# First attention of a four-layer block: where the causal mask is added, and wide score tiles in two pieces

## The chip, the cores and the metric

The kernel is one program on one core of a Trainium2 chip. The metric is the device time of one execution in microseconds. Engines named below: TensorE (PE) does matrix products and transposes, its operands come from SBUF and its results go to PSUM, which has eight banks of 512 float32 columns on each of 128 partitions; VectorE (DVE), ScalarE (ACT) and GpSimd (POOL) work element by element; SyncE (SP) issues the transfers. Each engine works through its own queue in order, and the queues are tied together by semaphores: an instruction waits until a semaphore has reached a number, and increments one when it is done.

## The reference

Four layers are applied to x of shape (2, 1024, 128), each as x + norm(layer(norm(x))), where norm is a layer norm without gain: an attention with rotary positions, a gated feed-forward of ternary weights, a differential attention with 8 heads, and a mixture of 8 experts. Only the first matters here:

```python
Q = jnp.einsum('btd,ed->bte', x, Wq)
K = jnp.einsum('btd,ed->bte', x, Wk)
V = jnp.einsum('btd,ed->bte', x, Wv)
Qr = _rotate(Q, cos, sin)
Kr = _rotate(K, cos, sin)
scores = jnp.einsum('bqd,bkd->bqk', Qr, Kr) / jnp.sqrt(jnp.float32(d))
mask = jnp.tril(jnp.ones((T, T), dtype=bool), k=1)
scores = jnp.where(mask[None, :, :], scores, -jnp.inf)
attn = jax.nn.softmax(scores, axis=-1)
out = jnp.einsum('bqk,bkd->bqd', attn, V)
```

The mask lets a query see all keys up to one beyond its own position (k=1). T is 1024 and d is 128.

## The kernel before

The first attention (stage a) works on 16 query tiles t of 128 rows, eight per batch; i = t mod 8 is the place of a tile in its batch. By the mask, tile i sees 128(i + 1) + 1 keys (at most 1024), so the width of its scores grows from 129 to 1024 columns. The scores of a tile lie in two neighbouring PSUM banks (0 and 1 for even t, 2 and 3 for odd t), so tiles with i of 4 and above reach well into the second bank, and tile i = 3 reaches into it by one column.

For each tile the work goes round four engines:

- TensorE, `a_scores(t)`: the product of rotated queries and keys, one per bank (L558), and over the last 129 columns (128 for i = 7) a product of a bfloat16 identity with the mask (L561), which adds -1e30 to the forbidden keys while the bank's accumulation is open. It waits for the rotation (`ropeq`, `ropek`) and for the exponentials of tile t - 2, which shared the banks.
- VectorE, `a_max(t)`: the row maximum over the whole width (L1322), then its multiple with the negative scale (L1323), the bias of the exponential.
- ScalarE, `a_exp(t)`: one exponential over the whole width with the row sum as a second output (L992).
- TensorE, `a_turn(t)`: i + 1 transposes of 128x128 into banks 4 and 5 (L574); ScalarE, `a_turned(t)`: a copy of them to SBUF (L1002); TensorE, `a_values(t)`: i + 1 products with the values (L587); VectorE, `a_next(t)` (L1334, L1335: the probability of the one key beyond the tile, and the reciprocal of the row sum) and `a_post(t)` (L1343, L1346: adding that key's value, and scaling the row).

The order on each engine is written out by hand. In step t TensorE does the scores of t, the transposes of t - 1 and the value products of t - 2; VectorE does `a_next(t - 2)`, `a_max(t)`, then `a_post(t - 2)`; ScalarE does the copy of t - 1 and the exponential of t. Into this order the remaining projections of the input (TensorE and ScalarE, t = 0 to 4), the rotation (VectorE at t = 0, 1, 4, 5, L1286 to L1307, and GpSimd for the second batch, L1849 and L1857) and the statistics and norms of finished rows (VectorE L1240 and L1243, GpSimd L1828 to L1831, ScalarE L979 after the exponentials of t = 7, 12, 13 and 15) are placed. `me.step` issues a VectorE instruction and waits for its end; `me.mark` issues it only. The helper `mm` is TensorE's matmul.

Of the kernel before, what the change touches and what calls it, by code (L numbers as in the profile page):

```python
# [18 lines left out]
BF16 = mybir.dt.bfloat16  # L19
I32 = mybir.dt.int32  # L20
ALU = mybir.AluOpType
# [3 lines left out]
P = 128  # L25
BATCH, SEQ = 2, 1024
TILES = BATCH * SEQ // P
BT = SEQ // P
# [114 lines left out]
def sandwich(nc, x_in, a_w, rope, b_w12, b_h1, b_h2, b_w3, b_s, b_s3, c_w, c_wo, c_bo, small,  # L143
             d_wg, d_wu, d_wd, d_wr, ident_in, ident_bf_in, mask_in, before_in, out):
    with ExitStack() as ctx:
        def sb(name, shape, dt=F32):
            return ctx.enter_context(nc.sbuf_tensor(name, shape, dt))
# [12 lines left out]
        ident = sb("ident", [P, P])  # L160
        ident_bf = sb("ident_bf", [P, P], BF16)
        mask = sb("mask", [P, P + 1], BF16)
# [42 lines left out]
        tiny = sb("tiny", [P, 64])  # L205
        nlam = sb("nlam", [P, 1])
        cs_tab = sb("cs_tab", [P, 2, CT, HEADS, 2])
        raw = sb("raw", [P, 2, CHUNK])
# [114 lines left out]
        def rotated(b, i):  # L323
# [3 lines left out]
            return 2 * b + (2 if P * (i + 1) < CHUNK else 3)  # L327

        def att_width(i):

            return min(P * (i + 1) + 1, SEQ)
# [28 lines left out]
        def _(sp):  # L360
# [6 lines left out]
            for c in range(2, CHUNKS):  # L367
                sp.dma_start(x[:, chunk(c), :], x_src[:, chunk(c), :]).then_inc(ld[f"x{c}"], 16)
            sp.dma_start(ident_bf[:], ident_bf_in).then_inc(ld["con"], 16)
            sp.dma_start(mask[:], mask_in).then_inc(ld["con"], 16)  # L370
# [117 lines left out]
        def _(pe):  # L488
# [46 lines left out]
            def a_scores(t):  # L535
                b, i = divmod(t, BT)
                base = 2 * (t % 2)
                if t == 0:
                    pe.wait_ge(ld["con"], 32)
                    pe.wait_ge(S["q_made"], 1)  # L540
                if t == 1:
                    pe.wait_ge(S["q_made"], 2)
                if t == 3:
                    pe.wait_ge(S["k_made"], 3)
                if t == 4:
                    pe.wait_ge(S["q_made"], CHUNKS)
                seen = rotated(b, i)
                pe.wait_ge(S["ropeq"], seen)
                pe.wait_ge(S["ropek"], seen)
                if t >= 2:  # L550
                    pe.wait_ge(S["e_a"], t - 1)
                w = att_width(i)
                for n0 in range(0, w, CHUNK):
                    n1 = min(w, n0 + CHUNK)
                    m0, m1 = max(n0, P * i), n1
                    bank = base + n0 // CHUNK
                    masked = m1 > m0
                    last = mm(ps[:, bank, 0:n1 - n0], q_t[:, b, i * P:(i + 1) * P], k_t[:, b, n0:n1],  # L558
                              start=True, stop=not masked)
                    if masked:  # L560
                        last = mm(ps[:, bank, m0 - n0:m1 - n0], ident_bf[:],  # L561
                                  mask[:, m0 - P * i:m1 - P * i], start=False, stop=True)
                last.then_inc(S["s_a"], 1)

            def a_turn(t):
                i = t % BT
                pe.wait_ge(S["e_a"], t + 1)
                if t == 0:
                    pe.wait_ge(S["vout"], 2)
                if t == 4:  # L570
                    pe.wait_ge(S["vout"], CHUNKS)
                pe.wait_ge(S["pe_a"], t)
                for j in range(i + 1):
                    last = nc.tensor.transpose(ps[:, 4 + j // CT, (j % CT) * P:(j % CT + 1) * P],  # L574
                                               probs[:, t % 2, j * P:(j + 1) * P], ident[:])
                last.then_inc(S["pt_a"], 1)
# [362 lines left out]
        def _(act):  # L939
# [46 lines left out]
            def a_exp(t):  # L986
                w = att_width(t % BT)
                act.wait_ge(S["m_a"], t + 1)
                if t >= 2:
                    act.wait_ge(S["pt_a"], t - 1)  # L990
                base = 2 * CHUNK * (t % 2)
                A(probs[:, t % 2, 0:w], banks[:, base:base + w], ACT.Exp, bias=nmx[:, t:t + 1],  # L992
                  scale=ATT_SCALE, accum_out=rsum[:, t:t + 1]).then_inc(S["e_a"], 1)

# [209 lines left out]
        def _(dve):  # L1204
# [113 lines left out]
            def a_max(t):  # L1318
                w = att_width(t % BT)
                dve.wait_ge(S["s_a"], t + 1)  # L1320
                base = 2 * CHUNK * (t % 2)
                me.step(v.tensor_reduce(mx[:, t:t + 1], banks[:, base:base + w], AX.X, ALU.max))  # L1322
                v.tensor_scalar(nmx[:, t:t + 1], mx[:, t:t + 1], -ATT_SCALE, None, ALU.mult).then_inc(S["m_a"], 1)  # L1323

# [4 lines left out]
            def a_next(t):  # L1329

                dve.wait_ge(S["e_a"], t + 1)
                w = P * (t % BT + 1)
                if t % BT < BT - 1:
                    me.mark(v.tensor_copy(p_next[:, t:t + 1], probs[:, t % 2, w:w + 1]))  # L1334
                me.step(v.reciprocal(rinv[:, t:t + 1], rsum[:, t:t + 1]))  # L1335

# [765 lines left out]
```

## Time and profile before

| | us |
|---|---|
| median of 3 runs (703.64 to 704.94) | 703.73 |
| the profiled execution | 704.66 |
| its span | 702.9 |
| TensorE busy | 634.1 |
| VectorE busy | 528.9 |
| ScalarE busy | 489.2 |
| GpSimd busy | 188.3 |

The span runs from the first to the last instruction that the profiler saw; the execution's time has a little around it. A row of a timeline has the start in us from the span's start, the duration in us (from the first start to the last end where several instructions are merged as xN), the engine, the line of the kernel, the operation, output and inputs by name with their shapes, and in brackets the idle time before it and what ended that. Neighbouring instructions on an engine can overlap a little, so that durations do not add up exactly. A row of the grouped view has the group's busy time, the mean duration of one in ns and the idle time before it. Of these, only the stretch up to about 72 us belongs to the first attention.

### The profile page before, as it was taken

What the parts mean: (1) busy time and instruction counts of PE and PEld (TensorE: products, weight loads), DVE (VectorE), ACT (ScalarE), POOL (GpSimd) and SP (SyncE); (2) the same over time, 40 slices, a digit from 0 to 9 for tenths busy, and PEclk for the clock granted to TensorE, in tenths of its full rate; (3) what the DMA queues carried; (4) which work ended last, traced back from release to release, by engine and by line L of the source; (5) the groups of instructions that cost most, each with busy time, mean ns of one, the idle gap of its engine ahead of it and who ended that gap; (6) DMA issues with size and microseconds to landing.
All of it is one profiled execution on the core that took longest, in us unless ns stands there. A gap on an engine that the chain in (4) does not pass through costs nothing.

```text
span 702.9 us, 9405 instructions
## 1 busy us (share of the span) xinstructions
PE 634.1 (90%) x3324; PEld 272.4 (39%) x3324; DVE 528.9 (75%) x993; ACT 489.2 (70%) x503; POOL 188.3 (27%) x250
## 2 busy tenths in 40 slices
PE   7989899999999899889988888898898788899996
PEld 4677345464464423223222112122231111266555
DVE  6876512427155399999899999999999999676775
ACT  4656324225333499999999999999999989444431
POOL 4532240212102041491148101705600006022012
PEclk9999999999999999999999999999999989999999
DMA  5430200002204301234013510111102103300171
GB/s 171 134 137 1 92 1 0 2 0 59 77 1 137 111 11 47 57 105 138 5 57 97 151 56 11 49 57 56 31 27 57 56 3 120 119 1 1 41 232 30
DMA packets 33230, 44.60 MB, mean 63 GB/s; under 512 B 5408, under 2 KB 20000, under 8 KB 32800
## 3 DMA queue, kind: packets, MB, share of 16 engines
q1 hardware_dynamic: 33184, 44.01, 21.1%
q8 instruction: 26, 0.43, 0.3%
q14 instruction: 20, 0.16, 0.1%
HBM read 31.60 MB, written 10.55 MB: 60 GB/s over the span
## 4 chain that ended last, share of the span: by engine, by line
PE 43%; ACT 23%; DVE 21%; issue 11%; POOL 1%; DVEq 0%; ACTq 0%
ACT w_hh L1138 19%; PE ps L778 8%; PE ps L788 8%; DVE hid L1482 5%; DVE hid L1477 5%; PE ps L813 5%; PE ps L760 4%; PE ps L690 3%; PE ps L671 3%; PE ps L744 2%; PE ps L822 2%; ACT probs L1109 2%; DVE st L1240 2%; PE ps L587 1%; PE ps L493 1%
## 5 line engine op out<-in xcount | busy, mean ns | idle before, releaser
L1138 ACT ACTIVATE w_hh<-hid 128x2048 f32<-128x2048 f32 x128 | 249.9, 1952 | 8.3 <-DVE hid L1482 7.8
L690 PE MATMUL ps<-w_hh,v_h 128*32 128x512 f32 x1024 | 137.8, 610 | 33.4 <-ACT w_hh L1138 32.3
L1477 DVE TENSOR_TENSOR hid<-ps,probs 128x1024 f32<-128x1024 f32 x86 | 104.5, 1215 | 19.4 <-ACT probs L1109 16.1
L671 PE MATMUL ps<-q_s,k_s 64*128 64x512 bf16 x256 | 99.3, 389 | 14.7 <-DVE hid L1477 14.1
L1482 DVE SCALAR_TENSOR_TENSOR hid<-ps,probs 128x1024 f32<-128x1024 f32 x86 | 104.7, 1217 | 4.6 <-PE ps L671 3.3
L671 PE MATMUL ps<-q_w,k_w 64*128 64x512 bf16 x256 | 99.4, 389 | 0.0
L1109 ACT ACTIVATE probs<-ps 128x1024 f32<-128x1024 f32 x86 | 91.3, 1062 | 2.2 <-PE ps L671 2.2
L671 PE MATMUL ps<-q_g,k_s 128*128 128x512 bf16 x256 | 78.3, 388 | 1.1 <-ACT qkv_a L1109 1.1
L671 PEld LDWEIGHTS ps<-q_w,k_w 64*128 64x128 bf16 x256 | 23.7, 92 | 107.2 <-issue 55.3
L788 PE MATMUL ps<-hid,w_hh 128*128 128x512 f32 x128 | 56.3, 592 | 0.0
L778 PE MATMUL ps<-hid,w_hh 128*128 128x512 f32 x128 | 55.8, 594 | 0.0
L1477 DVE TENSOR_TENSOR hid<-ps,qkv_a 128x1024 f32<-128x1024 f32 x42 | 51.0, 1215 | 2.7 <-ACT w_hh L1138 1.8
L1482 DVE SCALAR_TENSOR_TENSOR hid<-ps,qkv_a 128x1024 f32<-128x1024 f32 x42 | 51.2, 1218 | 2.0 <-PE ps L671 1.7
L1173 ACT ACTIVATE q_g<-ps 128x512 f32<-128x512 f32 x32 | 19.1, 598 | 45.5 <-PE ps L813 45.4
L671 PEld LDWEIGHTS ps<-q_s,k_s 64*128 64x128 bf16 x256 | 23.7, 92 | 63.2 <-DVE hid L1477 35.1
L1822 POOL TENSOR_SCALAR rs<-mv 128x4 f32<-128x4 f32 x18 | 5.2, 289 | 160.1 <-DVE mv L1243 160.0
L690 PEld LDWEIGHTS ps<-w_hh,v_h 128*32 128x32 f32 x1024 | 20.7, 108 | 69.1 <-ACT w_hh L1138 50.4
L1109 ACT ACTIVATE qkv_a<-ps 128x1024 f32<-128x1024 f32 x42 | 44.6, 1063 | 2.6 <-PE ps L671 2.6
L1379 DVE SCALAR_TENSOR_TENSOR hid<-ps,s_b,rot 128x512 f32<-128x512 f32 x16 | 11.9, 750 | 42.8 <-ACT rot L1075 42.8
L1093 ACT ACTIVATE hid<-ps,s_b 128x512 f32<-128x512 f32 x16 | 11.0, 687 | 43.9 <-PE ps L788 43.9
L1891 POOL TENSOR_SCALAR v_h<-v_c 128x128 f32<-128x128 f32 x16 | 8.5, 535 | 113.5 <-PE ps L690 113.4
L778 PEld LDWEIGHTS ps<-hid,w_hh 128*128 128x128 f32 x128 | 24.0, 190 | 30.2 <-issue 29.4
(314 smaller groups left out, 1001.2 us busy)
## 6 DMA issues: line engine op xcount, KB each, us to landing
qk_rows<-part SPq DMA_DIRECT2D x48, 128.0 KB, 2.4
w_hh<-w_rows SPq DMA_DIRECT2D x4, 1024.0 KB, 8.8
qk_rows<-part_g SPq DMA_DIRECT2D x24, 128.0 KB, 2.4
q_g<-qk_rows SPq DMA_DIRECT2D x32, 96.0 KB, 2.2
k_s<-qk_rows SPq DMA_DIRECT2D x32, 96.0 KB, 2.3
q_s<-qk_rows SPq DMA_DIRECT2D x32, 96.0 KB, 2.4
k_w<-qk_rows SPq DMA_DIRECT2D x32, 96.0 KB, 2.5
q_w<-qk_rows SPq DMA_DIRECT2D x32, 96.0 KB, 2.4
```

What stands on the lines that cost most here:

```text
L671: last = mm(ps[:, base + half, :], k_op[rows, u, keys], q_op[rows, u, half * CHUNK:(half + 1) * CHUNK], start=True, stop=True)
L690: last = mm(ps[VW * g4:VW * g4 + VW, 6, :], v_h[:, u, mt, :], ee[:, mt % 2, g4 * CHUNK:(g4 + 1) * CHUNK], start=(mt == 0), stop=(mt == BT ...
L744: last = mm(bank[:, k4 * P:(k4 + 1) * P], hid[:, 2, k, k4 * P:(k4 + 1) * P], w_3[:, k, :], start=(k == 0), stop=(k == KT_ - 1))
L760: last = mm(ps[:, 2 * (m % 2) + w, :], w_12[:, w, m * P:(m + 1) * P], xt[:], start=True, stop=True)
L778: last = mm(ps[:, o, :], w_h1[:, k, o * P:(o + 1) * P], hid[:, 0, k, :], start=(k == 0), stop=(k == KT_ - 1))
L788: last = mm(ps[:, o, :], w_h2[:, k, o * P:(o + 1) * P], hid[:, 1, k, :], start=(k == 0), stop=(k == KT_ - 1))
L813: last = mm(ps[:, 2 * (n % 2) + w, :], wt[:, e, :], xt_d[c], start=True, stop=True)
L1109: A(gg[s % 3], banks[:, 0:2 * CHUNK], ACT.Tanh).then_inc(S["g"], 1)
L1138: A(ee[:, mt % 2, :], zz[:, mt % 2, :], ACT.Exp).then_inc(S["e"], 1)
L1173: A(sg_d[:, n % 2, :], ps[:, 2 * (n % 2), :], ACT.Silu).then_inc(S["sg_d"], 1)
L1477: v.tensor_tensor(zz[:, mt % 2, 0:SEQ], banks[:, 2 * CHUNK:4 * CHUNK], gg[s % 3], ALU.add).then_inc(S["z1"], 1)
L1482: v.scalar_tensor_tensor(zz[:, mt % 2, SEQ:2 * SEQ], banks[:, 4 * CHUNK:6 * CHUNK], -1.0, gg[s % 3], ALU.mult, ALU.subtract).then_inc(S["z ...
```

## The change

The mask is no longer added by TensorE. VectorE adds it to the scores in PSUM, in place, over the last 128 or 129 columns, and then takes the maximum. The bfloat16 identity and its load go. Tiles with i of 4 and above are treated as two pieces, bank one and the rest: TensorE signals the first bank's product apart from the second's; VectorE takes one maximum of each piece and joins them in the operation that scales; ScalarE does two exponentials with a row sum each; TensorE's first four transposes wait for the first exponential only; VectorE adds the two row sums in `a_next`. The semaphores `s_a` and `e_a` now count pieces. The norms of this stage are on ScalarE in both versions.

```diff
+        mx_1, rsum_1 = tiny[:, 0:TILES], tiny[:, TILES:2 * TILES]
...
+        def pieces(t):
+
+            return 2 if t % BT >= CT else 1
+
+        def pieces_to(t):
+            return sum(pieces(u) for u in range(t + 1))
...
-            sp.dma_start(ident_bf[:], ident_bf_in).then_inc(ld["con"], 16)
...
-                    pe.wait_ge(ld["con"], 32)
...
-                    pe.wait_ge(S["e_a"], t - 1)
+                    pe.wait_ge(S["e_a"], pieces_to(t - 2))
                 w = att_width(i)
                 for n0 in range(0, w, CHUNK):
                     n1 = min(w, n0 + CHUNK)
-                    m0, m1 = max(n0, P * i), n1
-                    bank = base + n0 // CHUNK
-                    masked = m1 > m0
-                    last = mm(ps[:, bank, 0:n1 - n0], q_t[:, b, i * P:(i + 1) * P], k_t[:, b, n0:n1],
-                              start=True, stop=not masked)
-                    if masked:
-                        last = mm(ps[:, bank, m0 - n0:m1 - n0], ident_bf[:],
-                                  mask[:, m0 - P * i:m1 - P * i], start=False, stop=True)
+                    last = mm(ps[:, base + n0 // CHUNK, 0:n1 - n0], q_t[:, b, i * P:(i + 1) * P], k_t[:, b, n0:n1],
+                              start=True, stop=True)
+                    if n0 == 0 and pieces(t) == 2:
+                        last.then_inc(S["s_a"], 1)
                 last.then_inc(S["s_a"], 1)
...
-                pe.wait_ge(S["e_a"], t + 1)
+                pe.wait_ge(S["e_a"], pieces_to(t) - pieces(t) + 1)
...
                 for j in range(i + 1):
+                    if j == CT:
+                        pe.wait_ge(S["e_a"], pieces_to(t))
...
-                A(probs[:, t % 2, 0:w], banks[:, base:base + w], ACT.Exp, bias=nmx[:, t:t + 1],
-                  scale=ATT_SCALE, accum_out=rsum[:, t:t + 1]).then_inc(S["e_a"], 1)
+                for i, total in enumerate((rsum, rsum_1)[0:pieces(t)]):
+                    n0, n1 = i * CHUNK, w if i == pieces(t) - 1 else CHUNK
+                    A(probs[:, t % 2, n0:n1], banks[:, base + n0:base + n1], ACT.Exp, bias=nmx[:, t:t + 1],
+                      scale=ATT_SCALE, accum_out=total[:, t:t + 1]).then_inc(S["e_a"], 1)
...
             def a_max(t):
                 w = att_width(t % BT)
-                dve.wait_ge(S["s_a"], t + 1)
                 base = 2 * CHUNK * (t % 2)
-                me.step(v.tensor_reduce(mx[:, t:t + 1], banks[:, base:base + w], AX.X, ALU.max))
-                v.tensor_scalar(nmx[:, t:t + 1], mx[:, t:t + 1], -ATT_SCALE, None, ALU.mult).then_inc(S["m_a"], 1)
+                if pieces(t) == 2:
+                    dve.wait_ge(S["s_a"], pieces_to(t) - 1)
+                    me.mark(v.tensor_reduce(mx_1[:, t:t + 1], banks[:, base:base + CHUNK], AX.X, ALU.max))
+                n0 = CHUNK * (pieces(t) - 1)
+                dve.wait_ge(S["s_a"], pieces_to(t))
+                if t == 0:
+                    dve.wait_ge(ld["con"], 16)
+                seen = banks[:, base + P * (t % BT):base + w]
+                me.step(v.tensor_tensor(seen, seen, mask[:, 0:w - P * (t % BT)], ALU.add))
+                me.step(v.tensor_reduce(mx[:, t:t + 1], banks[:, base + n0:base + w], AX.X, ALU.max))
+                if pieces(t) == 2:
+                    v.tensor_scalar(nmx[:, t:t + 1], mx[:, t:t + 1], mx_1[:, t:t + 1], -ATT_SCALE,
+                                    ALU.max, ALU.mult).then_inc(S["m_a"], 1)
+                else:
+                    v.tensor_scalar(nmx[:, t:t + 1], mx[:, t:t + 1], -ATT_SCALE, None, ALU.mult).then_inc(S["m_a"], 1)
...
-                dve.wait_ge(S["e_a"], t + 1)
+                dve.wait_ge(S["e_a"], pieces_to(t))
                 w = P * (t % BT + 1)
                 if t % BT < BT - 1:
                     me.mark(v.tensor_copy(p_next[:, t:t + 1], probs[:, t % 2, w:w + 1]))
+                if pieces(t) == 2:
+                    me.step(v.tensor_tensor(rsum[:, t:t + 1], rsum[:, t:t + 1], rsum_1[:, t:t + 1], ALU.add))
                 me.step(v.reciprocal(rinv[:, t:t + 1], rsum[:, t:t + 1]))
```

What stands on VectorE in the step t = 7, before: `a_next(5)`, `a_max(7)`, `a_post(5)` (mx is the maximum, nmx its scaled negative, rsum the row sum, rinv its reciprocal).

```order
L1334 COPY p_next<-probs 128x1 [waits e_e_a]
L1335 RECIPROCAL rinv<-rsum 128x1
L1322 TENSOR_REDUCE mx<-ps 128x1 [waits e_s_a,self_dve]
L1323 TENSOR_SCALAR nmx<-mx 128x1 [waits self_dve]
L1343 SCALAR_TENSOR_TENSOR y_a<-hid,p_next,ps 128x128 [waits e_v_next0,e_o_a]
L1346 TENSOR_SCALAR y_a<-y_a,rinv 128x128 [waits self_dve]
```

And in the changed kernel, where tiny holds the first piece's maximum and the second piece's row sum:

```order
L1351 COPY p_next<-probs 128x1 [waits e_e_a]
L1353 TENSOR_TENSOR rsum<-rsum,tiny 128x1
L1354 RECIPROCAL rinv<-rsum 128x1 [waits self_dve]
L1328 TENSOR_REDUCE tiny<-ps 128x1 [waits e_s_a,self_dve]
L1334 TENSOR_TENSOR ps<-ps,mask 128x128 [waits e_s_a]
L1335 TENSOR_REDUCE mx<-ps 128x1 [waits self_dve]
L1337 TENSOR_SCALAR nmx<-mx,tiny 128x1 [waits self_dve]
L1362 SCALAR_TENSOR_TENSOR y_a<-hid,p_next,ps 128x128 [waits e_v_next0,e_o_a]
L1365 TENSOR_SCALAR y_a<-y_a,rinv 128x128 [waits self_dve]
```

Three instructions are new: the addition of row sums, the second maximum and the mask's addition. Tiles with i below 4 get the mask's addition only.

On TensorE, the rows around the transposes of t = 7, before: the scores of t = 8, the transposes, the value products of t = 6.

```order
L558 MATMUL ps<-qkv_a 128x129 [waits e_e_a,e_ropek,e_ropeq]
L561 MATMUL ps<-mask,ident_bf 128x129
L574 MATMUL ps<-ident,probs 128x128 [waits e_pe_a,e_e_a]
L574 MATMUL ps<-ident,probs 128x128 x7
L587 MATMUL ps<-qkv_a,probs_t 128x128 [waits e_y_a,e_pe_a]
```

And in the changed kernel:

```order
L560 MATMUL ps<-qkv_a 128x129 [waits e_e_a,e_ropek,e_ropeq]
L577 MATMUL ps<-ident,probs 128x128 [waits e_pe_a,e_e_a]
L577 MATMUL ps<-ident,probs 128x128 x3
L577 MATMUL ps<-ident,probs 128x128 [waits e_e_a]
L577 MATMUL ps<-ident,probs 128x128 x3
L590 MATMUL ps<-qkv_a,probs_t 128x128 [waits e_y_a,e_pe_a]
```

The mask product is gone, and the eight transposes have two waits for ScalarE instead of one.

## Rows read from the trace of the kernel before

**Rows 1.** Windows: us, busy us of each engine (instructions), granted PE clock, DMA.

```profile
14.00:28.00 14.00, 12.55 (x65) 7.93 (x64) 11.91 (x39) 11.48 (x29) 7.18 (x10) 1.00 0.33 82
28.00:42.00 14.00, 13.16 (x88) 9.97 (x86) 13.34 (x39) 7.48 (x14) 8.25 (x9) 1.00 0.82 275
52.00:62.00 10.00, 9.39 (x56) 6.76 (x57) 8.13 (x36) 8.26 (x19) 2.39 (x6) 1.00 0.00 1
```

**Rows 2.** Timeline of VectorE, 14 to 45 us.

```profile
21.74 1.29 DVE L1301 TENSOR_TENSOR qkv_a<-qkv_a,sq 128x512 f32<-128x512 f32 x2
...
27.28 0.35 DVE L1343 SCALAR_TENSOR_TENSOR y_a<-hid,p_next,ps 128x128 f32<-128x128 f32 x1 [1.65 <-PE ps L587]
...
28.83 0.14 DVE L1334 COPY p_next<-probs 128x1 f32<-128x1 f32 x1
...
40.87 0.15 DVE L1323 TENSOR_SCALAR nmx<-mx 128x1 f32<-128x1 f32 x1
```

**Rows 3.** Grouped view by shape, VectorE: xcount | busy us, mean ns | idle.

```profile
L1335 DVE RECIPROCAL rinv<-rsum 128x1 f32<-128x1 f32 x16 | 2.4, 152 | 0.0
L1322 DVE TENSOR_REDUCE mx<-ps 128x1 f32<-128x1024 f32 x2 | 2.4, 1224 | 0.1
L1322 DVE TENSOR_REDUCE mx<-ps 128x1 f32<-128x129 f32 x2 | 0.6, 292 | 0.0
L1561 DVE TENSOR_TENSOR probs_t<-qkv_a,r_o 128x128 f32<-128x128 f32 x2 | 0.5, 283 | 0.0
L1298 DVE TENSOR_TENSOR raw<-ps,tab 128x258 f32<-128x258 f32 x2 | 0.8, 416 | 0.0
```

**Rows 4.** Timeline of TensorE, 14 to 25 us.

```profile
15.87 0.22 PE L561 MATMUL ps<-mask,ident_bf 128*128 128x129 bf16 x1
...
22.78 0.39 PE L587 MATMUL ps<-qkv_a,probs_t 128*128 128x128 f32 x2
23.29 1.10 PE L558 MATMUL ps<-qkv_a 128*128 128x512 f32 x2
24.22 0.22 PE L561 MATMUL ps<-mask,ident_bf 128*128 128x128 bf16 x1
24.28 0.33 PE L558 MATMUL ps<-qkv_a 128*128 128x1 f32 x2
```

**Rows 5.** Timelines of GpSimd and VectorE where one holds up the other.

```profile
34.50 2.88 POOL L1857 TENSOR_TENSOR qkv_a<-qkv_a,part 128x512 f32<-128x512 f32 x2 [0.85 <-DVE part L1307]
...
35.31 0.93 DVE L1346 TENSOR_SCALAR y_a<-y_a,rinv 128x128 f32<-128x128 f32 x1
...
37.99 0.29 DVE L1346 TENSOR_SCALAR y_a<-y_a,rinv 128x128 f32<-128x128 f32 x1
...
55.93 0.24 POOL L1828 TENSOR_SCALAR nb<-mv 128x4 f32<-128x4 f32 x1 [3.17 <-DVE mv L1243]
...
62.01 0.66 DVE L1327 TENSOR_TENSOR x_res<-x_res,y_a 128x512 f32<-128x512 f32 x1
...
62.19 0.58 POOL L1828 TENSOR_SCALAR nb<-mv 128x4 f32<-128x4 f32 x1 [4.31 <-DVE mv L1243]
```

**Rows 6.** Timeline of ScalarE, 27 to 68 us.

```profile
27.36 0.69 ACT L992 ACTIVATE probs<-ps,nmx 128x513 f32<-128x513 f32 x1
27.94 0.21 ACT L992 ACTIVATION_READ_ACCUMULATOR probs<-ps,nmx 128x1 f32 x1
...
41.06 1.11 ACT L992 ACTIVATE probs<-ps,nmx 128x1024 f32<-128x1024 f32 x1 [0.25 <-DVE nmx L1323]
...
42.16 1.64 ACT L979 ACTIVATE y_a<-y_a,nb,rs 128x128 f32<-128x128 f32 x4
...
67.06 1.00 ACT L1002 ACTIVATE probs_t<-ps 128x1024 f32<-128x1024 f32 x1
```

**Rows 7.** Timeline of TensorE, 42 to 70 us.

```profile
42.32 1.09 PE L574 MATMUL ps<-ident,probs 128*128 128x128 f32 x8 [0.84 <-ACT probs L992]
...
58.20 0.87 PE L574 MATMUL ps<-ident,probs 128*128 128x128 f32 x6
...
66.60 3.56 PE L587 MATMUL ps<-qkv_a,probs_t 128*128 128x128 f32 x30
```

**Rows 8.** Timeline of VectorE near 64 us; waits up to 160 us (total, times, longest).

```profile
64.22 0.15 DVE L1323 TENSOR_SCALAR nmx<-mx 128x1 f32<-128x1 f32 x1
...
PEld ps L574 <- ACT probs L992: 6.1, 8, 1.8
...
DVE mx L1322 <- PE ps L561: 0.5, 2, 0.3
```

More of the change, by code:

```diff
@@ L143, in sandwich @@
 def sandwich(nc, x_in, a_w, rope, b_w12, b_h1, b_h2, b_w3, b_s, b_s3, c_w, c_wo, c_bo, small,
-             d_wg, d_wu, d_wd, d_wr, ident_in, ident_bf_in, mask_in, before_in, out):
+             d_wg, d_wu, d_wd, d_wr, ident_in, mask_in, before_in, out):
     with ExitStack() as ctx:
@@ L160, in sandwich @@
         ident = sb("ident", [P, P])
-        ident_bf = sb("ident_bf", [P, P], BF16)
         mask = sb("mask", [P, P + 1], BF16)
@@ L2089 @@
         "d_wd": f["L1_ffn_Wd"].transpose(1, 0, 2), "d_wr": f["L1_ffn_Wr"], "ident": eye,
-        "ident_bf": eye.astype(ml_dtypes.bfloat16), "mask": mask, "before": before,
+        "mask": mask, "before": before,
     }
```

## The prediction

> **What bounds the kernel now.** The change touches the first attention alone, so I asked first where that stage lies and which engine it waits for. It runs over 16 query tiles (t = 0 to 15, eight per batch) from about 16 us to 70 us of the span. The windows view is the first to read: between 28 and 42 us VectorE is busy for 13.34 of 14.00 us, while in 52 to 62 us it is TensorE with 9.39 of 10.00 and VectorE has 8.13 [rows 1]. The timeline of VectorE is the second: from 28.83 us on (the small operations ahead of the maximum of t = 4) up to the end of the scaled maximum of t = 7 at 41.02 us not one row has an idle time behind it [rows 2]. So tiles 4 to 7 run at VectorE's pace, tiles 8 to 15 at that of a ring (scores on TensorE, maximum on VectorE, exponentials on ScalarE, transposes on TensorE) with TensorE nearly full. Behind the stage the order of all engines is unchanged and the next stage starts from the last products, so what the stage loses or gains reaches the end one to one. The granted TensorE clock is 1.00 in every window of the stage [rows 1], so the clock enters neither side.
>
> **The start, t = 0 to 3: +0.4 us.** Each tile gets one VectorE addition of 128x129 in PSUM. No row of before has that form. From below: the slope between the maxima of 129 and 1024 columns is (1224 - 292) / 895 = 1.04 ns a column, and 129 columns at that rate alone are 0.13 us; with the 0.03 us that VectorE takes from one finished operation to a dependent next one, 0.165. From above: an addition of 258 columns out of PSUM, 0.416 us, with the same 0.03, 0.45. I take the nearest in size, an SBUF product of 128x128 at 283 ns, with 0.03: **0.31 us** [rows 3]. (The Trainium skill, Vector Engine (DVE) Microarchitecture Reference, 5.2 Measured stream behaviour on trn2, gives about 75 ns of fixed cost per instruction after overlap, an estimate of 0.21 us here; by it the sum below would be about 1.0 us smaller. The rows speak for more: the 292 ns of the 129-column maximum leave 158 beside its columns, and each addition here is waited for.) The additions of t = 0 and 1 stand ahead of the rotation of rows 512 to 1023, which ends at 23.03 us, and the scores of t = 3 start at 23.29 us on it [rows 2, 4]. That is +0.62, less 0.12 of slack (TensorE's product before ends at 23.17 us), so 0.5; the two mask products of t = 3 go, 0.08 us of TensorE. The value products of t = 1 then end 0.4 later, and VectorE, idle 1.65 us for them [rows 2], absorbs the additions of t = 2 and 3 (0.62).
>
> **Tiles 4 to 7, VectorE's own pace: +2.0 us.** Per tile: the mask addition, 0.31; a second maximum over the same columns in all, which costs its fixed part of 292 - 129 x 1.04 = 158 ns less the 0.07 to 0.08 by which undependent operations overlap, 0.08. Four tiles: 4 x 0.39 = 1.6. In the steps of t = 6 and 7 the sums of the exponentials of t = 4 and 5 are in two parts, and their addition lies between a copy and the reciprocal: an operation of one column, 152 ns as the reciprocal, and 0.03 [rows 3], 0.18 each, 0.36 for two. Nothing covers these, since VectorE has no idle there. That the first maximum may start while TensorE writes the second bank brings nothing here: VectorE comes late to both.
>
> **A port that is held, t = 6: +1.1 us.** At 34.50 us GpSimd starts two additions of 128x512 that end at 37.38 us. VectorE's 128x128 scaling at 35.31 us takes 0.93 us instead of 0.29 and ends when the first of the two has ended; and VectorE's two-input addition at 62.01 us stretches a GpSimd operation from 0.24 to 0.58 us [rows 5]. So operations with two SBUF inputs are among those that exclude GpSimd's. The new addition of t = 4's two sums has two SBUF inputs and comes at 36.30 us in before's time, when GpSimd's second has just begun: it waits until 37.38, 1.1 us, in a stretch without slack. (The Trainium skill, GPSIMD Engine Reference, 1. Specifications, says the same of "two SBUF inputs"; the trace shows it with VectorE as the holder, not yet with one column.) Rows cannot tell whether one column suffices: zero is the other end.
>
> **The handover to the second batch, t = 8 to 11: +0.6 us.** An exponential of 513 columns takes 0.69 us and its sum is out 0.79 us after the start [rows 6]; so with a piece of 512 the transposes of t = 7 can start 0.84 us after 41.06 instead of 1.26 (42.32 [rows 7]). Four of them fill 0.44 us, but the second piece ends at 0.70 + 0.79 = 1.49, so all eight are done at 1.98 instead of 2.19: 0.2 us won. ScalarE pays for it, 1.49 instead of 1.22 us, 0.27, then it does the norm of 1.64 us that stands at 42.16 us [rows 6], and only then the copy of t = 7's transposes and the exponential of t = 8, for which the transposes of t = 8 wait. That returns the 0.2 and 0.1 more. The masks of t = 8 to 10 leave TensorE (0.06 each); the VectorE additions of t = 10 and 11 (0.62), with other VectorE work in between and no idle, stand ahead of the exponential of t = 11. Sum: 0.1 - 0.1 + 0.6.
>
> **The second half, t = 12 to 15: +0.9 us.** TensorE sets the pace, and VectorE's additions of 0.39 first use its idle. At t = 13 the scaled maximum comes 0.40 later, the first piece of the exponential is ready 0.84 us on, and the transposes at 58.20 us [rows 7] end 0.24 later than now. At t = 15 the scaled maximum, now at its end at 64.37 us [rows 8], is late by 0.24 + 0.18 + 0.40 = 0.82. Then ScalarE: two pieces (+0.27), the norm, and the copy of the last transposes from 67.06 us [rows 6] is late by 1.09, so it ends at 69.15. The products on t = 14 (14 of the 30 from 66.60 us [rows 7]) end at about 68.2 now and 68.8 then, so the last 16 wait for that copy: they start at 69.2 instead of 68.25, +0.9.
>
> The dropped load of an identity (32 KB) and its place in the DMA queue are worth nothing: the first mask product runs at 15.87 us [rows 4], behind other work; the mask is in by then.
>
> **The sum.** 0.4 + 2.0 + 1.1 + 0.6 + 0.9 = 5.0 us. The profiled execution took 704.66 us, so it would take 709.7; the median of the runs is 703.73, 0.93 lower, so I predict **708.7 us**.
>
> **Rivals.**
> - *No port wait.* One column does not need GpSimd's port: the sum is 3.9, the time 707.6. For it: rows with one column on VectorE are short everywhere. Against it: the rule is in the kind of operation, not its length.
> - *The addition is dear.* If an operation that reads and writes PSUM costs the upper end (0.45), ten such additions on the path (t = 0, 1, 4 to 7, 10, 11, 13, 15) add 10 x 0.14: 710.1.
> - *The addition is cheap* (0.165): 10 x 0.145 less, 707.2, or 706.1 with no port wait.
> - *Faster: TensorE and the handovers set everything.* The 18 mask products leave TensorE (0.06 us each, as between the starts at 24.22 and 24.28 us, 1.0 in all [rows 4]), the wait of the maxima for them goes (0.5 us [rows 8]), and the handovers of t = 7 and 15 shorten by 0.2 each: 1.9 less, 701.8. For it: TensorE is at 9.39 of 10.00 us in the second half [rows 1], and it waits 6.1 us in all for exponentials [rows 8]. It decides only if VectorE had over 2 us to spare between 28.83 and 41.02 us, and there it has none.
>
> **How the numbers follow.** The forecast has 0.40, no port wait 0.24, dear 0.11, cheap 0.12, faster or level 0.13. A change within 0.2% (1.4 us) can't be told from none. Slower holds all cases but the last: 0.87. The last is split, since VectorE's cost may use up most of that gain: faster 0.08, same 0.05. The range reaches from the cheap case with some of the handover won, 705.3, to just above the dear one, 710.4. Leaving out 701.8 costs 0.13.
>
> **What would show each step.** In the profile after: mask additions of 0.28 to 0.32 us, sixteen; the scores of t = 3 at about 23.8 us; the scaled maximum of t = 7 ending near 44.5 (41.02 + 3.5); one one-column addition of about 1.2 us against seven of 0.15; the last copy out of the transposes ending near 73.3; the stage's last product near 75 instead of 70.2. I am wrong if VectorE shows idle times over 0.2 us in tiles 4 to 7, if the addition is under 0.2 us, or if the following stage starts no later than now.

## The result and the profile after

| | before | after |
|---|---|---|
| median of 4 runs each, us | 704.34 (703.64 to 704.98) | 710.61 (709.40 to 711.76) |
| the profiled execution, us | 704.66 | 711.76 |
| its span, us | 702.9 | 709.9 |

The changed kernel is slower: the ratio is 1.0093, with an interval of [1.0078, 1.0107]. The forecast was 708.7 us with a range up to 710.4. The direction and the places were right; the time is 1.9 us above the forecast and 0.2 us outside the range. Three single executions in the runs below took 891, 1217 and 3400 us; they are left out of every median, and the one of them that was profiled (in r_after) gives no rows.

The page of the kernel after, its first two lines (span; busy time of each engine, share, instructions):

```profile
span 709.9 us, 9416 instructions
...
PE 636.7 (90%) x3306; PEld 273.5 (39%) x3306; DVE 537.2 (76%) x1025; ACT 491.2 (69%) x519; POOL 187.9 (26%) x250
```

VectorE has 8.3 us more than before (537.2 against 528.9). Windows of the kernel after (columns as in [rows 1]): the stretch of tiles 4 to 7, then the end of the stage.

```profile
28.00:45.00 17.00, 13.82 (x85) 9.90 (x84) 16.24 (x47) 8.21 (x20) 9.07 (x10) 1.00 0.67 227
...
72.00:73.00 1.00, 1.00 (x9) 1.00 (x8) 0.00 (x0) 1.00 (x4) 0.00 (x0) 0.67 0.05 16
73.00:74.00 1.00, 1.00 (x7) 1.00 (x7) 0.00 (x0) 0.97 (x2) 0.00 (x0) 0.50 0.00 0
74.00:75.00 1.00, 1.00 (x6) 1.00 (x6) 0.00 (x0) 0.00 (x0) 0.00 (x0) 0.50 0.00 0
75.00:76.00 1.00, 1.00 (x8) 1.00 (x7) 0.80 (x4) 0.00 (x0) 0.00 (x0) 0.62 0.00 0
```

The stretch that took 14 us now takes 17, and VectorE is busy for 16.24 of them: it is still the engine that sets the pace there. New is the last column but two of the lower rows: the granted TensorE clock, 1.00 in the same stage of the kernel before, is 0.50 (1.2 instead of 2.4 GHz) from 73 to 75 us.

VectorE of the kernel after, grouped by shape (as [rows 3]):

```profile
L1334 DVE TENSOR_TENSOR ps<-ps,mask 128x129 f32<-128x129 f32 x14 | 4.1, 295 | 0.5 <-PE ps L560 0.2
...
L1353 DVE TENSOR_TENSOR rsum<-rsum,tiny 128x1 f32<-128x1 f32 x8 | 2.2, 279 | 0.0
...
L1337 DVE TENSOR_SCALAR nmx<-mx,tiny 128x1 f32<-128x1 f32 x8 | 1.7, 214 | 0.3
...
L1340 DVE TENSOR_SCALAR nmx<-mx 128x1 f32<-128x1 f32 x8 | 1.2, 154 | 0.3
```

The mask's addition takes 0.295 us. The scaling that also joins the two maxima takes 0.214 us where the plain one takes 0.154. The addition of two row sums has a mean of 0.279 us, which hides one long one. Timeline of VectorE and GpSimd, 36 to 45 us, where one holds up the other (against [rows 2, 5]):

```profile
36.24 2.88 POOL L1876 TENSOR_TENSOR qkv_a<-qkv_a,part 128x512 f32<-128x512 f32 x2 [1.30 <-DVE part L1312]
...
37.97 1.17 DVE L1353 TENSOR_TENSOR rsum<-rsum,tiny 128x1 f32<-128x1 f32 x1
...
42.83 0.15 DVE L1353 TENSOR_TENSOR rsum<-rsum,tiny 128x1 f32<-128x1 f32 x1
...
44.87 0.21 DVE L1337 TENSOR_SCALAR nmx<-mx,tiny 128x1 f32<-128x1 f32 x1
```

At t = 6 the one-column addition takes 1.17 us and ends at 39.14 us, 0.02 us behind the second of GpSimd's two operations (36.24 + 2.88 = 39.12). The next one, with GpSimd idle, takes 0.15.

TensorE of the kernel after at the scores of t = 3, the transposes of t = 7 and the end of the stage (against [rows 4, 7]), then ScalarE at the exponentials of t = 7 and the last copy (against [rows 6]):

```profile
24.27 1.21 PE L560 MATMUL ps<-qkv_a 128*128 128x512 f32 x4 [0.86 <-DVE qkv_a L1306]
...
45.95 1.32 PE L577 MATMUL ps<-ident,probs 128*128 128x128 f32 x8 [1.31 <-ACT probs L997]
...
70.92 1.32 PE L577 MATMUL ps<-ident,probs 128*128 128x128 f32 x8 [1.88 <-ACT probs L997]
72.08 5.14 PE L590 MATMUL ps<-qkv_a,probs_t 128*128 128x128 f32 x30
77.74 0.66 PE L499 MATMUL ps<-ident,xn 128*128 128x128 f32 x4 [0.52 <-DVE y_a L1365]
```

```profile
45.12 0.69 ACT L997 ACTIVATE probs<-ps,nmx 128x512 f32<-128x512 f32 x1 [1.08 <-DVE nmx L1337]
...
45.80 0.68 ACT L997 ACTIVATE probs<-ps,nmx 128x512 f32<-128x512 f32 x1
...
46.46 1.64 ACT L982 ACTIVATE y_a<-y_a,nb,rs 128x128 f32<-128x128 f32 x4
...
72.97 1.01 ACT L1007 ACTIVATE probs_t<-ps 128x1024 f32<-128x1024 f32 x1
```

In the kernel before, TensorE's transposes of t = 15 and those that start the next stage (L493 there) are:

```profile
65.67 1.09 PE L574 MATMUL ps<-ident,probs 128*128 128x128 f32 x8 [1.59 <-ACT probs L992]
...
70.68 0.66 PE L493 MATMUL ps<-ident,xn 128*128 128x128 f32 x4 [0.52 <-DVE y_a L1346]
```

The last 30 value products take 5.14 us instead of 3.56, in just the stretch with the low clock. The next stage starts with its transposes (L499) at 77.74 us; before, they start at 70.68. Behind that nothing changes: TensorE is busy for 78.64 of 80 us from 73 to 153 us before and from 80 to 160 us after, and the spans differ by 7.0 us, as the starts of the stage behind do by 7.06.

**How the kernels below are compared.** Three points of the timeline cut the stage: the scores of t = 3 (23.29 us before [rows 4]), the scaled maximum of t = 7 (40.87 [rows 2]) and the next stage's transposes (70.68). The first moves by some tenths from execution to execution with the input's transfer: VectorE's statistics of x, which wait for it, start anywhere from 11.35 to 12.30 us in the profiles of this study. The two stretches behind it repeat to 0.02 us where nothing in them is changed (20.60 to 20.62 and 31.74 in the rows below that alter neither), so each can be read apart. The columns of times are in us.

| kernel | scores t = 3 | from there to the scaled maximum of t = 7 | from there to the next stage | low clock at the end |
|---|---|---|---|---|
| before | 23.29 | 17.58 | 29.81 | no |
| after | 24.27 | 20.60 | 32.87 | yes |
| after, second profile (r_after2) | 24.07 | 20.61 | 31.74 | no |
| e_ident | 23.96 | 20.61 | 31.74 | no |
| e_mask | 24.45 | 18.76 | 32.60 | yes |
| e_pieces | 23.38 | 19.41 | 30.46 | no |
| e_port | 23.81 | 19.69 | 32.94 | yes |
| e_twice | 24.60 | 21.93 | 33.31 | no |
| e_warm | 24.30 | 20.61 | 32.35 | no |
| e_warm2 | 24.33 | 20.62 | 31.74 | no |
| e_psum | 23.94 | 16.65 | 30.03 | no |
| e_late | 23.64 | 17.57 | 28.94 | no |
| e_best | 23.20 | 16.65 | 29.09 | no |

### The profile page after: what moved, and what is told of

It is laid out like the page before. It is cut to its first block, busy times and chain, and to the rows that moved or that the text cites. A ratio compares the mean times of both kernels' runs of the same rounds, so it can differ in the third digit from the quotient of the medians.

```text
span 709.9 us, 9416 instructions
## 1 busy us (share of the span) xinstructions
PE 636.7 (90%) x3306; PEld 273.5 (39%) x3306; DVE 537.2 (76%) x1025; ACT 491.2 (69%) x519; POOL 187.9 (26%) x250
## 4 chain that ended last, share of the span: by engine, by line
PE 41%; DVE 25%; ACT 22%; issue 11%; POOL 1%; DVEq 0%; ACTq 0%
ACT w_hh L1143 17%; PE ps L781 8%; PE ps L791 8%; DVE hid L1496 6%; DVE hid L1501 6%; PE ps L816 5%; PE ps L763 4%; PE ps L693 3%; PE ps L674 2%; PE ps L747 2%; PE ps L825 2%; DVE st L1245 2%; ACT probs L1114 1%; PE ps L590 1%; PE ps L499 1%
## 5 line engine op out<-in xcount | busy, mean ns | idle before, releaser
L1501 DVE SCALAR_TENSOR_TENSOR hid<-ps,probs 128x1024 f32<-128x1024 f32 x86 | 104.6, 1217 | 3.9 <-PE ps L674 2.7
```

Source lines behind the costliest of these rows:

```text
L1501: v.scalar_tensor_tensor(zz[:, mt % 2, SEQ:2 * SEQ], banks[:, 4 * CHUNK:6 * CHUNK], -1.0, gg[s % 3], ALU.mult, ALU.subtract).then_inc(S["z ...
```

## The experiments

Twelve runs, in three groups, two of them of the changed kernel itself. The kernel before was run beside each group, with medians of 704.44 (r_after to e_port), 704.35 (e_warm, e_twice, e_psum, e_ident) and 703.74 us (the other four).

**r_after: the changed kernel once more**, as the neighbour of the next three.

> The changed kernel once more, unaltered. Two theories on the 1.3 us by which it was slower than the sum of 5.0. Clock: TensorE's granted clock falls to 0.50 behind the idle time ahead of the transposes of t = 15 and makes the last products of the stage 1.6 us longer (5.14 instead of 3.56 us); where the fall is missing, the execution is 1.6 us shorter. Work: VectorE's and ScalarE's additions cost more than the terms; then the time is the same with or without the fall. Both: ratio to before 1.008 to 1.010. The start of the scores of t = 0, 0.35 us later in the first profile (16.00 against 15.65), is back within 0.1 of before if it was chance in the input's transfer.

Measured: 711.63 us (three executions, 710.66 to 711.88), ratio 1.0093 [1.0077, 1.011]. It has no rows.

**e_mask: the mask on VectorE, no pieces.**

```diff
 def pieces(t):
-    return 2 if t % BT >= CT else 1
+    return 1
```

> The mask addition on VectorE alone: every tile one piece, as before. By my terms: start +0.4, tiles 4 to 7 4 x 0.31 = +1.25, no port wait, t = 8 to 11 +0.6 (no second piece on ScalarE, but VectorE's additions at t = 10 and 11), t = 12 to 15 +0.5: together +2.7 us, ratio 1.004, the scaled maximum of t = 7 ending 1.7 later than before. Rival (the pieces are what costs): +1 us or less.

Measured: 707.84 us, ratio 1.004 [1.0028, 1.0053]: 3.4 us by the medians, 2.8 by the ratio. By the table the stretch up to the scaled maximum of t = 7 is 1.18 longer, a little under four additions with their gaps (4 x 0.325 = 1.30). The end of the stage, TensorE's timeline:

```profile
69.22 1.09 PE L577 MATMUL ps<-ident,probs 128*128 128x128 f32 x8 [1.99 <-ACT probs L997]
70.15 5.14 PE L590 MATMUL ps<-qkv_a,probs_t 128*128 128x128 f32 x30
```

So the low clock does not need the pieces. Its 30 products took the 5.14 us of the kernel after, 1.58 more than before's 3.56. Without that the last stretch would be 31.02, 1.21 longer than before, since the copy that the last 16 read ends 1.46 us after the first product starts (71.61 and 70.15), as it does in the kernel before (68.06 and 66.60), where nothing waits for it.

**e_pieces: the pieces, with the mask still on TensorE.**

```diff
+                    if masked:
+                        last = mm(ps[:, bank, m0 - n0:m1 - n0], ident_bf[:],
+                                  mask[:, m0 - P * i:m1 - P * i], start=False, stop=True)
...
-                me.step(v.tensor_tensor(seen, seen, mask[:, 0:w - P * (t % BT)], ALU.add))
```

> The two pieces alone, the mask on TensorE as before. By my terms: start 0, tiles 4 to 7 4 x 0.08 + 2 x 0.18 + 4 x 0.06 for the scaling with two pointers = +0.9, port wait +1.1, handover -0.2 to +0.3, end +0.4: +2.2 to +2.7 us, ratio 1.0035. Rival (the pieces pay by the shorter handovers, the mask is what costs): 0 or faster. The rest that the two parts alone leave of the whole 6.3 would be what comes of both together, the clock first of all.

Measured: 706.54 us, ratio 1.0029 [1.002, 1.0038]. The middle stretch is 1.83 longer, the last 0.65. VectorE, then TensorE at the end:

```profile
36.55 1.17 DVE L1358 TENSOR_TENSOR rsum<-rsum,tiny 128x1 f32<-128x1 f32 x1
```

```profile
67.57 1.32 PE L586 MATMUL ps<-ident,probs 128*128 128x128 f32 x8 [1.49 <-ACT probs L1006]
68.74 1.73 PE L599 MATMUL ps<-qkv_a,probs_t 128*128 128x128 f32 x14
70.68 2.05 PE L599 MATMUL ps<-qkv_a,probs_t 128*128 128x128 f32 x16 [0.22 <-ACT probs_t L1016]
```

The hold of 1.17 us belongs to the pieces, and so does a wait that before has not: the last 16 products start 0.22 us late, on ScalarE's copy (L1016). The two halves of the change add up: in the middle stretch 1.18 + 1.83 = 3.01 against 3.03 for both, in the last 1.21 + 0.65 = 1.86 against 1.93.

**e_port: the row sums added by an instruction with one stream**, the second sum being its scalar pointer.

```diff
-me.step(v.tensor_tensor(rsum[:, t:t + 1], rsum[:, t:t + 1], rsum_1[:, t:t + 1], ALU.add))
+me.step(v.tensor_scalar(rsum[:, t:t + 1], rsum[:, t:t + 1], rsum_1[:, t:t + 1], None, ALU.add))
```

> The changed kernel with the two row sums added by an operation that takes the second as a per-partition scalar, so that it has one tensor input in SBUF. Port theory: the addition of t = 4's sums takes 0.15 instead of 1.17 us beside GpSimd's second addition, the scaled maximum of t = 7 ends 1.0 us earlier, the time falls by 1.0 us. Rival (the 1.17 us is a wait for something else, or the time is given back at the copy of the transposes): same as the changed kernel within 0.3.

Measured: 709.43 us, ratio 1.0068 [1.0053, 1.0083]; 1.2 us under the changed kernel's 710.61 and 2.2 under the runs beside it. The table says it better: the middle stretch is 0.91 shorter than in the kernel after, and the last is equal to it (32.94 and 32.87, both with the low clock). VectorE:

```profile
37.51 0.20 DVE L1353 TENSOR_SCALAR rsum<-rsum,tiny 128x1 f32<-128x1 f32 x1
```

Same place (GpSimd's two operations run from 35.78 to 38.66 us here), same data, and 0.20 us instead of 1.17 (the rest of its eight pay 0.05 more each). The hold of this operation comes from the second SBUF stream, not from where the instruction stands. The Trainium skill (GPSIMD Engine Reference, 1. Specifications) names "two SBUF inputs" as one of the two cases of contention; the trace agrees, and adds that one column is enough and that the pointer scalar of this operation doesn't count as the second input. A single SBUF tensor is no safe form in general: the 128x128 scaling just ahead (L1365, one tensor and a pointer) takes 0.92 us at 36.60 us in this kernel too, against 0.29 with GpSimd idle.

**e_ident: the dropped load of the identity kept.**

```diff
+            sp.dma_start(ident_bf[:], ident_bf_in).then_inc(ld["con"], 16)
...
-                    dve.wait_ge(ld["con"], 16)
+                    dve.wait_ge(ld["con"], 32)
```

> The changed kernel with the load of the bfloat16 identity kept (nobody reads it). I put the dropped load at nothing: the same time as the changed kernel within 0.5 us. Rival (its place in the queue moved the input's third transfer, which the profile after shows 0.2 us later): 0.3 us faster.

Measured: 709.92 us, ratio 1.0083 [1.0068, 1.0098]; both stretches equal to the second profile of the changed kernel, and the scores of t = 3 at 23.96 us, among those of the kernels with one mask addition and without the load (23.81 to 24.45). The load is worth nothing that shows.

**e_twice: the mask's addition done twice.** A forbidden score gets -2e30 instead of -1e30, and its exponential is zero either way.

```diff
-                me.step(v.tensor_tensor(seen, seen, mask[:, 0:w - P * (t % BT)], ALU.add))
+                for _ in range(2):
+                    me.step(v.tensor_tensor(seen, seen, mask[:, 0:w - P * (t % BT)], ALU.add))
```

> The changed kernel with each mask addition made twice, one behind the other (the forbidden scores get -2e30 instead of -1e30, which changes no output). It prices one addition where it stands. By my terms the second costs what the first did: 0.32 each at t = 0 and 1, 4 to 7, 10 and 11, 13 and 15, ten places, +3.2 us; the scaled maximum of t = 7 ends 1.9 later. Rival (most of the additions lie in VectorE's idle times and the cost of the change is the waits and the clock): +1 us or less.

Measured: 713.29 us, ratio 1.013 [1.0116, 1.0143]: 3.4 us over e_ident of the same group, 2.7 over 710.61. The middle stretch grows by 1.32, four times 0.33; the last by 1.57, between four and five times 0.33 for the eight additions in it. So an addition costs its duration and a gap of 0.03 in full where VectorE sets the pace (t = 4 to 7), and for a little over half of the additions behind that. TensorE waited longest of all here, and the clock stayed high:

```profile
74.17 1.32 PE L577 MATMUL ps<-ident,probs 128*128 128x128 f32 x8 [2.21 <-ACT probs L997]
75.33 1.73 PE L590 MATMUL ps<-qkv_a,probs_t 128*128 128x128 f32 x14
```

**e_warm: four products in TensorE's idle time before the transposes of t = 15**, to keep the clock up.

```diff
+                if t == TILES:
+                    pe.wait_ge(S["e_a"], pieces_to(TILES - 2))
+                    for _ in range(4):
+                        mm(ps[:, 0, :], k_t[:, 1, 0:P], k_t[:, 1, 0:CHUNK], start=True, stop=True)
```

> The changed kernel with four matmuls of 512 columns, whose result nobody reads, on TensorE between the value products of t = 13 and the wait for the first exponential of t = 15, where it stood idle 1.88 us. Clock theory: TensorE's granted clock stays 1.00 there, the 30 last value products take 3.6 instead of 5.14 us, the time falls by 1.4 to 1.6 us (the four take 1.72 us, within the idle time). Rival (the chip lowers the clock at this point for what ran before, or the last products are slow for another reason): the same time, 5 us for the products.

Measured: 710.66 us, ratio 1.0093 [1.0079, 1.0106]. TensorE:

```profile
68.92 3.60 PE L614 MATMUL ps<-qkv_a 128*128 128x512 f32 x8
...
73.23 3.51 PE L590 MATMUL ps<-qkv_a,probs_t 128*128 128x128 f32 x30
```

The experiment was badly sized: a float32 product of 512 columns is two instructions of 0.45 us, so the four filled 3.60 us instead of half of that, and the transposes came 1.4 us late. The clock stayed at 1.00, but that proves little.

**e_warm2: the same with two products**, which fit: 1.88 us, then the transposes 0.17 us behind them.

> As the run with four matmuls on TensorE ahead of the transposes of t = 15, with two. Each had turned out as two instructions of 0.45 us, so that the four took 3.60 us instead of the 1.72 that I had allowed for and made these transposes 1.4 us late; two take 1.8 us, inside the 1.88 of idle time. The granted clock stayed 1.00 and the 30 products took 3.51 us there. Clock theory: the clock stays 1.00, the transposes are not late, and the time is 1.0 to 1.6 us below the changed kernel run beside it (1.6 where each of its executions has the fall, less where some have not). Rival: no difference, the fall being a matter of chance that hits both.

Measured: 710.17 us, ratio 1.0087 [1.0073, 1.01]. The clock was high, and the last stretch is 31.74, to the hundredth that of the changed kernel without the fall; its time is 0.3 us above that one's (r_after2, below), inside the noise. Filling the idle costs nothing in the stage. Whether it keeps a fall away is not shown, since the profile beside it had none.

**r_after2: the changed kernel, in the same group.**

> The changed kernel again, beside the one above. One profile of it had the fall of the clock (0.50 from 72.4 to 75.6 us), another, with one unused load more, had none and a stage 5.6 us longer than before's instead of 6.7. Clock theory: ratio to before 1.008 to 1.010, and, if the profile shows no fall, the first product of the next stage 5.6 us after before's (76.3), if it does, 7.1 (77.8).

Measured: 709.86 us (709.22 to 711.45), ratio 1.0084 [1.007, 1.0098]. TensorE, and a window:

```profile
70.75 1.32 PE L577 MATMUL ps<-ident,probs 128*128 128x128 f32 x8 [1.88 <-ACT probs L997]
71.91 1.73 PE L590 MATMUL ps<-qkv_a,probs_t 128*128 128x128 f32 x14
73.86 2.05 PE L590 MATMUL ps<-qkv_a,probs_t 128*128 128x128 f32 x16 [0.22 <-ACT probs_t L1007]
76.42 0.66 PE L499 MATMUL ps<-ident,xn 128*128 128x128 f32 x4 [0.52 <-DVE y_a L1365]
```

```profile
72.00:74.00 2.00, 1.78 (x16) 1.59 (x15) 0.27 (x1) 1.80 (x4) 0.00 (x0) 1.00 0.03 8
```

The same program, the same idle of 1.88 us, and no fall. The wait of the last 16 products for the copy is here as forecast. So the fall is a matter of the execution. In the changed kernel it costs 32.87 - 31.74 = 1.13 us, less than the 1.6 of the products, since without it these would wait for the copy.

**e_psum: the kernel before, with its rows kept in PSUM between `a_post`'s two instructions.** The scaling then reads PSUM and not SBUF.

```diff
-                    me.step(v.scalar_tensor_tensor(y_a[:, t, :], v_next[:, b, i, :], p_next[:, t:t + 1], o,
+                    me.step(v.scalar_tensor_tensor(o, v_next[:, b, i, :], p_next[:, t:t + 1], o,
...
-                    o = y_a[:, t, :]
```

> The kernel before with one thing changed: the row before scaling (values plus the one key beyond) goes back to PSUM instead of SBUF, so that the scaling reads PSUM. Port theory: the scaling then does not wait for GpSimd's additions: 0.35 instead of 1.25, 0.93 and 0.93 us at t = 3 to 5, and 0.06 dearer in the eleven other tiles. VectorE sets the pace there, so the scaled maximum of t = 7 ends 1.2 to 2.0 us earlier, and the kernel is faster than before by 0.8 to 1.5 us (TensorE has under 1 us to spare there). Rival (TensorE or ScalarE takes over at once, or the PSUM operation waits too): no change within 0.3.

Measured: 703.41 us against 704.35, ratio 0.999 [0.9981, 0.9999]. VectorE:

```profile
31.65 0.35 DVE L1345 TENSOR_SCALAR y_a<-ps,rinv 128x128 f32<-128x128 f32 x1
...
32.53 0.96 DVE L1322 TENSOR_REDUCE mx<-ps 128x1 f32<-128x769 f32 x1 [0.41 <-PE ps L561]
```

The scaling takes 0.35 us at t = 3 to 5, where it takes 0.9 to 1.25 in the kernel before (0.93 in [rows 5]). The middle stretch is 0.93 shorter, though some 2 us of VectorE were freed: the rest became waits for TensorE, the 0.41 above among them. 0.22 of it is given back in the last stretch, so the stage gains 0.7 us, a little under the 0.8 to 1.5 that had been expected.

**e_late: the kernel before, with the statistics and the addition of finished rows moved from VectorE's step 14 to 15, and the last norm on ScalarE behind the last copy.**

```diff
-                if t == 15:
+                if t == TILES:
...
-                if t in (6, 12, 14):
+                if t in (6, 12, 15):
...
-                if t in (8, 14, 17):
+                if t in (8, 15, 17):
```

> The kernel before with the statistics of the rows of t = 8 to 11 and the addition of those of t = 4 to 7 moved on VectorE behind the maximum of t = 15 (from t = 14 to 15), and their norm on ScalarE behind the copy of the last transposes. Ring theory: the scaled maximum of t = 15 then ends about 1.9 us earlier (1.2 of statistics, 0.7 of addition), the exponential of t = 15 is held by the copy of t = 14's transposes instead (63.7), 0.7 us earlier than now, and the kernel is 0.6 to 0.8 us faster. Rival (the stage's last products are held by what moved behind): same within 0.3.

Measured: 703.68 us against 703.74, ratio 0.9992 [0.9983, 1.0001]. In the table the last stretch is 0.87 shorter; the timing, with its interval from -1.2 to +0.1 us, doesn't settle it, and the 0.6 to 0.8 us expected of it stay open.

**e_best: both edits on the kernel before.**

> The same, and the rows before scaling kept in PSUM as in the run that was 0.1% faster: the two gains lie in different halves of the stage and add up: 1.2 to 1.6 us below before, ratio 0.998. Rival: the one takes the other's slack, and the ratio is that of the better alone.

Measured: 702.72 us (701.86 to 703.52, ten runs) against 703.74, ratio 0.9978 [0.9969, 0.9988]. TensorE:

```profile
63.98 1.09 PE L574 MATMUL ps<-ident,probs 128*128 128x128 f32 x8 [0.76 <-ACT probs L992]
...
68.94 0.65 PE L493 MATMUL ps<-ident,xn 128*128 128x128 f32 x4 [0.52 <-DVE y_a L1345]
```

The wait of the last transposes falls from 1.59 to 0.76 us, and the next stage starts 1.74 us earlier than in the kernel before: 0.93 in the middle stretch, 0.72 in the last, 0.09 by the start. It is faster than the kernel before by 0.1 to 0.3%, and so than both kernels.

## Why the prediction was right in its mechanism and wrong in its size

**What bounds the kernel.** Right: tiles 4 to 7 run at VectorE's pace (16.24 of 17.00 us), and what was added to VectorE there is paid nearly in full (1.18 of 1.30 us in e_mask, 1.32 of 1.32 in e_twice). Behind the stage all was shifted one to one.

**The steps that failed** are two: a term put at nothing, and a sum that was too small. The first is the last sentence of the prediction's part on what bounds the kernel: "The granted TensorE clock is 1.00 in every window of the stage [rows 1], so the clock enters neither side." The rows were those of the kernel before, and the conclusion was drawn for both. The mechanism forecast for the end of the stage has TensorE idle ahead of the transposes of t = 15 for longer than the 1.59 us of before; it stood idle for 1.88, and in the profiled execution the clock went to 0.50 between 1 and 2 us after work had begun again. A cost above zero belonged in the range there. In this execution it was 1.13 us. The fall of this one execution is not the whole miss: less 1.13 us it would take 710.63, and the median of the four would be 710.45, still just outside the range. The second step is the sum of the terms, +5.0 us, where the rows without a fall show +5.64; the table below has it by terms. The Trainium skill (TensorE: Matmul & The Clock Gate, Part 1) says that the phase at which the chip looks at activity is not tied to the program and varies from run to run; that fits one program with and without the fall, though no run here shows the cause.

How much of the median it makes is only suggested. Of twelve executions of the changed kernel, three have a mean clock of 0.991 and times of 711.63 to 711.88 us; nine have 0.996 or 0.997 and a median of 710.16. No execution of the kernel before, of 50, is below 0.993. But the mean clock is a weak mark: e_port's profiled execution has the fall at a mean of 0.996, and e_warm's has none at 0.993.

**The terms.** The rows without the fall (31.74) against the forecast:

| term | forecast | measured |
|---|---|---|
| start, up to the scores of t = 3 | +0.4 (scores +0.5) | +0.68 |
| tiles 4 to 7, with the port | +2.0 + 1.1 = 3.1 | +3.03 |
| handover, t = 8 to 11 | +0.6 | +0.76 |
| t = 12 to 15 | +0.9 | +1.17 |
| sum | +5.0 | +5.64 |

- *The price of the mask's addition*: taken 0.31 with its gap, measured 0.295 + 0.03. Right, and both rivals on it (0.45 and 0.165) are out; that the time of the dear one, 710.1, lies nearest the result is chance. The Trainium skill's fixed cost of about 75 ns (Vector Engine (DVE) Microarchitecture Reference, 5.2) gave 0.21; the measurement decides against it for an instruction that is waited for: e_twice shows 0.33 for each further one.
- *The port*: right in place and size (1.17 us for an operation of 0.15, a hold of 1.02 where 1.1 was forecast); e_port takes it away and wins 0.91. The rival without it is out.
- *The start*: measured as the mean of the scores of t = 3 in the seven profiles with one mask addition on VectorE (24.17) less that in the five without (23.49). Counted from the start of VectorE's statistics of x, which takes the input's transfer out, it is 0.69 (12.31 to 12.51 us against 11.63 to 11.93). Two additions with their gaps are 0.65. The forecast took off 0.12 of slack, which the profile of before has and those with a later input don't, and 0.08 for mask products, which lie behind this point.
- *The slack at t = 3*: VectorE's idle of 1.65 us [rows 2] was filled by more than the two additions. The scaling of t = 1 now takes 1.09 us (at 25.55 us, beside GpSimd) instead of 0.29, and of the idle 0.1 us is left at 28.12. Nothing of that 0.8 reaches the total, but the forecast's 0.62 was not all that the slack had to bear.
- *The pieces' joining*: the scaling that takes the other maximum as a pointer scalar takes 0.06 us more than the one with immediates only (0.214 against 0.154). I had it at nothing. It stands on the path at t = 4 to 7, and where the path passes VectorE again in t = 12 to 15. In tiles 4 to 7 its 0.24 doesn't show in the total; there the mask's additions came to 1.18 (e_mask) instead of 1.24 and the hold to 1.02 instead of 1.1.
- *Handover*: the transposes of t = 7 start 0.83 us after their exponential (forecast 0.84). The exponential of t = 11 starts 11.67 us after the scaled maximum of t = 7 instead of 10.91 (+0.76). Between the scaled maxima of t = 7 and t = 11, e_mask is 0.54 longer than before and e_pieces 0.15. Both are near their parts of the forecast (0.5 and 0.1); the rest of the 0.76 is not separated. One thing that no term has is the addition of t = 7's two row sums (50.18 us), ahead of the maximum of t = 9.
- *The end*: from the scaled maximum of t = 11 to that of t = 15 the changed kernel is 0.86 longer (forecast 0.82). From there to the next stage it is 0.29 longer (6.75 in r_after2, 6.46 before), where the forecast's 0.9 left 0.08. That is the pieces' as well (6.76 in e_pieces): the last copy is late by 0.29 us more than the scaled maximum, where 0.27 was forecast, but it is paid whole and not for the most part hidden behind the products on t = 14. The wait of the last 16 products for it is there.
- *The marks of the prediction*: the mask additions, the hold and the start of the next stage are as it said. The times are each later by the terms above: the scores of t = 3 at 24.27 us (23.8), the scaled maximum of t = 7 ending at 45.08 (44.5), the last copy at 73.98 (73.3).

**The rest of the miss.** The forecast was laid on a median of 703.73 us; 50 later runs of the kernel before have 704.15, so 0.4 us of the 1.9 are the base. With 0.6 of terms that leaves 0.9 for the fall of the clock and the chance of the input's transfer, which the runs don't separate. Each of the three is more than the 0.2 us by which the median lies outside, so no single one made the miss.

**The faster rival** asked for more than 2 us of spare time on VectorE between 28.83 and 41.02 us. It has none, e_mask and e_pieces both lose, and the wait of TensorE's weight loads for exponentials grew from 6.1 us [rows 8] to 12.8 (waits view of the kernel after, up to 80 us):

```profile
PEld ps L577 <- ACT probs L997: 12.8, 13, 2.6
```

**What stays open**: why some executions show the fall and others don't. Three of the profiles with an idle of 1.88 us or more had it (1.88, 1.93, 1.99), three didn't (1.88 twice, 2.21); none of those with 1.66 or less did. No kernel was found whose idle alone decides.

## What to carry to other kernels

Work taken off the busiest engine by average can land on the engine that sets the pace of one stretch: ask for each stretch which engine has no idle behind its rows, and charge whatever is added there at full duration plus its gap. Beside a busy GpSimd, look at the form of small VectorE operations: a second SBUF input can cost the rest of GpSimd's instruction even for one column (1.17 us here). A pointer scalar avoided that in the one-column addition, but the 128x128 scaling that has one was held as well (0.92 us), and a source in PSUM freed it (0.35). A clock that is full in the profile of before says nothing of a change that lengthens TensorE's waits; give it a price in the range.

## What the runs showed of the hardware

- A VectorE operation of one column with two SBUF inputs took 1.17 us beside a GpSimd operation of 128x512, 0.15 us without it, and 0.20 us in the form with a pointer, at the same place.
- A 128x128 scaling beside GpSimd's additions took 0.35 us out of PSUM and 0.93 to 1.25 out of SBUF in the same place.
- Adding 129 columns in place in PSUM took 0.295 us.
- In one of two profiles of the same program TensorE's clock fell to 0.50 behind an idle of 1.88 us, and 30 products took 5.14 us instead of 3.56 to 4.0.
- The start of the first work on the input's second part moved between 11.35 and 12.30 us from execution to execution, with nothing changed ahead of it in most of these kernels.
